# Latent attention with the rotated dimensions in three blocks of 64, two heads to a query tile, and the context product on quarters of the array

## The chip, the cores and the metric

The kernel runs on one core of one Trainium2 chip. Its engines are TensorE (PE, with its weight loads PEld), VectorE (DVE), ScalarE (ACT), GpSimd (POOL) and SyncE (SP, which only issues loads here). The metric is the device time of one execution in microseconds (us). Lower is better.

## The reference

The reference is a two-layer block over x (4 batches of 256 rows, 256 wide) and a context of 4 x 256 rows, 64 wide. The first layer has a top-k attention against the context and a routed feed-forward layer. The second has a latent attention and a mixture of experts. Only the latent attention is touched here. For each of its H = 16 heads, in words:

```
q     = norm(x) @ Wq_h.T                    # 128 wide
c     = q @ w_kc_q_h                        # 192 wide, latent query
c     = rope(c)                             # 192 dimensions: pairs (j, j + 96) are turned
qc    = c @ W_qr_h @ W_kr_h.T               # back to the 64 of the context
p     = softmax(qc @ rope(ctx).T)
out  += (p @ ctx') @ (w_kc_kv_h, Wo_h)      # folded
```

The rotation is x * cos + rotate_half(x) * sin with halves of 96 dimensions.

## The kernel before, in words

The weights of a pair of heads are folded first, so that the rows of x see one product less: `CH`, `CL` (Wq times w_kc_q, as two f16 parts, 256 x 2 x 192), `M` (W_qr times W_kr, 96 x 4 x 64) and `NH`, `NL` (w_kc_kv times Wo). `fold_product`, `fold_keep` and `fold_rest` (L135 to L182) do this in six parts, f = 0 to 5, through one PSUM bank; f = 0, 1 and 5 are split in two f16 parts, the high part by ACT and the remainder by DVE. `load_pair` (L188) issues 7 loads per pair from SP. The folds of pairs 0 and 1 run in the first stage (`stage_first_layer`), those of pair p+2 during pair p.

`stage_latent_attention` (L792) works through 8 pairs of heads. A pair has 8 steps t, one for each tile of 128 rows of x. Each engine has its own instruction list in a fixed order, joined by semaphores. All of them follow `pairs` (L840): steps 2 to 7 of a pair by `step`, and steps 0 and 1 of the next pair by `cross`; six pairs run in a hardware loop (`Fori`, two pairs a turn, three turns), the last two are written out.

In a step, PE does in this order:

- `scores` (L899) of tile t: two heads, against `KH` and `KL`, four f16 matmuls of 256 columns.
- `queries` (L875) for the next pair: group t of 8. A group is one head, one half of 96 dimensions and 512 rows of x: six f16 matmuls of 512 columns into 96 rows of bank 0 or 1. It waits for the rotation of the group before last.
- at steps 1 and 6 `to_context` (L888): from the rotated queries `RO` (96 rows) and `M` to 64 rows per head, four f32 matmuls of 512 columns, the two heads on the two column halves of the array, into bank 2. It serves half of the rows of x, so a pair has two calls.
- from step 3 on one part of the fold of pair p+2, the sixth in `cross` at step 0, through bank 7.
- at 3, 5, 7 and at the next pair's step 1 `attend` (L916), f32, and last `turn` (L908), four f32 transposes of the softmax rows of the tile before.

DVE does in a step: `lowest` (L1108, the minimum of the scores), the Q remainders and fold remainders where they fall, `rotate` (L1073, two products of a query group with cos and sin, 96 x 512 each, read from PSUM), `attended` (L1101) and last `inverse` (L1114), the reciprocal of the sum of the exponentials. The rotation thus stands between the minimum and the inverse, while ACT makes the exponentials (`softmax`, L986, two instructions with a sum read after each). ACT also copies Q (`to_context`, L980), the folds, the turned rows (`turned`, L995) and the attended context. POOL multiplies by the inverse (`normalise`, L1052) and adds and subtracts the rotated parts (`rotated`, L1044, two instructions after each second step), with two sets of `TM`.

The rope tables `cosq` and `sinq` are 96 x 2 x 256 each and come by two loads (L311, L312) in the first stage, ahead of three loads for the shared expert (L314) and of the loads of pairs 0 and 1.

Of the kernel before, what the change touches and what calls it, by code (L numbers as in the profile page):

```python
# [14 lines left out]
ALU = mybir.AluOpType  # L15
# [119 lines left out]
def fold_product(pe, g, u, f, o):  # L135

    if f < 2:
        for h in range(2):
            mm = pe.matmul(o[:, h * DQ:(h + 1) * DQ], g.WQ[u][:, h, f * P:(f + 1) * P], g.WCQ[u][:, h, :],
                           start=True, stop=True)  # L140
    elif f == 2:
        for h in range(2):
            pe.transpose(o[:, h * HALF:(h + 1) * HALF], g.WQR[u][:, h, :, :].rearrange("j a r -> j (a r)"),
                         g.ident[0:HALF, 0:HALF])
        mm = pe.transpose(o[:, 2 * HALF:2 * HALF + DC], g.WKR[u][:, :, :].rearrange("d h r -> d (h r)"),
                          g.ident[0:DC, 0:DC])
    elif f == 3:
        for h in range(2):
            for c in range(KT):
                mm = pe.transpose(o[:, h * D + c * P:h * D + (c + 1) * P], g.WO[u][:, c, h * HK:(h + 1) * HK],  # L150
                                  g.ident[:, :])
    elif f == 4:
        for h in range(2):
# [10 lines left out]
def fold_keep(act, g, r, u, f, o):  # L164
# [3 lines left out]
    if f == 2:  # L168
        act.activation(g.RT[:, 0, :], o[0:R, 0:2 * HALF + DC], ACT.Copy)
        return act.activation(g.RT[:, 1, :], o[R:P, 0:2 * HALF + DC], ACT.Copy)  # L170
    if f == 3:
        return act.activation(g.WOT[:, :, :], o, ACT.Copy)
    if f == 4:
        return act.activation(g.M[u][:, :, :], o[0:HALF, 0:4 * DC], ACT.Copy, scale=1.0 / UP)
# [10 lines left out]
DW = 7 * 16  # L185


def load_pair(sp, g, i, r, u):  # L188

    two_heads = bass.ds(2 * r, 2)  # L190
    wqr_v = i["L1_xattn_W_qr"].rearrange("h (a j) r -> j h a r", a=2)
    sp.dma_start(g.WQ[u][:, :, :], i["L1_xattn_Wq"].rearrange("(h k) n -> k h n", k=HK)[:, two_heads, :]
                 ).then_inc(g.d_w[u], 16)
    sp.dma_start(g.WCQ[u][:, :, :], i["L1_xattn_w_kc_q"].rearrange("h k q -> k h q")[:, two_heads, :]
                 ).then_inc(g.d_w[u], 16)
    sp.dma_start(g.WCV[u][:, :, :], i["L1_xattn_w_kc_kv"].rearrange("h k d -> k h d")[:, two_heads, :]
                 ).then_inc(g.d_w[u], 16)
    for h in range(2):
        sp.dma_start(g.WQR[u][:, h, :, :], wqr_v[:, bass.ds(2 * r + h, 1), :, :]).then_inc(g.d_w[u], 16)
# [6 lines left out]
def stage_first_layer(nc, g, i):  # L206
# [8 lines left out]
    with ExitStack() as ctx:  # L215
# [64 lines left out]
        fold_bank = lambda k: g.ps[:, (N_FOLD + k) % 4, :]  # L280

# [11 lines left out]
        with nc.Block() as block:  # L293
            @block.sync
            def _(sp):
# [15 lines left out]
                sp.dma_start(g.cosq[:, :, :], i["cosq"]).then_inc(g.d_ropeq, 16)  # L311
                sp.dma_start(g.sinq[:, :, :], i["sinq"]).then_inc(g.d_ropeq, 16)  # L312
# [64 lines left out]
            def _(pe):  # L377
# [91 lines left out]
                def fold(k):  # L469
# [6 lines left out]
                    fold_product(pe, g, r, f, fold_bank(k)).then_inc(filled, 1)  # L476
# [82 lines left out]
            def _(act):  # L559
# [41 lines left out]
                for n in range(3):  # L601
                    act.activation(g.shT[:, n, :, :], bank(N_SH + n), ACT.Copy,
                                   scale=UPW if n == 2 else 1.0).then_inc(emptied, 1)
                def fold(k):
# [3 lines left out]
                    if f in FOLD_SPLIT:  # L608
                        w = 2 * DQ if f < 2 else D
                        fold_keep(act, g, r, r, f, o).then_inc(fold_a, 1)  # L610
# [4 lines left out]
                    else:  # L615
                        fold_keep(act, g, r, r, f, o).then_inc(emptied, 1)
# [175 lines left out]
def stage_latent_attention(nc, g, i):  # L792
# [12 lines left out]
    with ExitStack() as ctx:  # L805
# [4 lines left out]
        TM = two("TM", [HALF, 4, 512])  # L810
        RO = sb("RO", [HALF, 2, 2, 2, 512])
# [9 lines left out]
        FIRST, AHEAD = 5, 6  # L821
        QA, QP, SC, PTB, CXB, FO = 0, 2, 3, 5, 6, 7
# [7 lines left out]
        EXP0, ROPE0, TPS0, TOK0, CXPS0, CXOK0, QC0, QCPS0, SUM0, FOLD0 = 2, 2, 2, 1, 2, 1, 1, 2, 4, 1  # L830
# [9 lines left out]
        def pairs(eng, step, cross):  # L840

            for t in HEAD:
                step(0, 0, t, True, False)
            with eng.Fori(0, (PAIRS - 2) // 2, 1) as it:
                for u in range(2):
                    for t in TILES:
                        step(it * 2 + u, u, t, True, True)
                    for t in HEAD:
                        cross(it * 2 + (u + 1), 1 - u, t, True, True)
            for t in TILES:  # L850
                step(PAIRS - 2, 0, t, True, False)
            for t in HEAD:
                cross(PAIRS - 1, 1, t, False, False)
            for t in TILES:
                step(PAIRS - 1, 1, t, False, False)

        with nc.Block() as block:
# [9 lines left out]
            def _(pe):  # L867
                def fold(r, u, f):
# [4 lines left out]
                    fold_product(pe, g, u, f, g.ps[:, FO, :]).then_inc(fold_ps, 1)  # L873

                def queries(q, u, t):  # L875

                    n, h, a = t // 4, t // 2 % 2, t % 2
                    pe.wait_ge(rope_ok, 8 * q + (t - 1 + ROPE0))
                    pe.wait_ge(fold_ok, 6 * q + (2 + FOLD0))
                    for k in range(KT):  # L880
                        for m, (cx, xx) in enumerate(split(g.CH[u], g.CL[u], g.XH, g.XL)):
                            mm = pe.matmul(g.ps[0:HALF, QA + a, :],  # L882
                                           cx[:, k, h * DQ + a * HALF:h * DQ + (a + 1) * HALF],
                                           xx[:, k, 512 * n:512 * n + 512], start=(k == 0 and m == 0),
                                           stop=(k == KT - 1 and m == 2))
                    mm.then_inc(q_ps, 1)

                def to_context(q, u, n):  # L888

                    pe.wait_ge(sum_ok, 8 * q + (4 * n + 4 + SUM0))  # L890
                    pe.wait_ge(fold_ok, 6 * q + (5 + FOLD0))
                    pe.wait_ge(qc_ok, 2 * q + (n + QC0))
                    for a in range(2):
                        for h in range(2):
                            mm = pe.matmul(g.ps[DC * h:DC * h + DC, QP, :], g.M[u][:, 2 * h + a, :],  # L895
                                           RO[:, n, h, a, :], start=(a == 0), stop=(a == 1))
# [32 lines left out]
                def step(p, u, t, asks, folds):  # L929
                    scores(p, u, t)  # L930
                    if asks:
                        queries(p + 1, 1 - u, t)
                    else:
                        shares(t)
                    if t == 1:
                        to_context(p, u, 1)
                    if t == AHEAD and asks:
                        to_context(p + 1, 1 - u, 0)
                    if folds and t >= 3:
                        fold(p + 2, u, t - 3)  # L940
# [5 lines left out]
                def cross(p, u, t, asks, folds):  # L946

                    scores(p, u, t)
                    if asks:
                        queries(p + 1, 1 - u, t)  # L950
                    else:
                        if t == 0:
                            pe.wait_ge(rope_ok, 8 * PAIRS + ROPE0)
                            pe.wait_ge(cx_ok, 4 * p - 2 + CXOK0)
                        shares(t)
                    if t == 0:
                        if folds:
                            fold(p + 1, 1 - u, FOLDS - 1)
                        turn(p - 1, LAST)
                    else:  # L960
                        to_context(p, u, 1)
# [4 lines left out]
                for t in range(NT):  # L966
                    queries(0, 0, t)
                    if t == FIRST:
                        to_context(0, 0, 0)
# [5 lines left out]
            def _(act):  # L975
                def fold(r, u, f):
                    act.wait_ge(fold_ps, 6 * r + (f + 1))
                    fold_keep(act, g, r, u, f, g.ps[:, FO, :]).then_inc(fold_hi if f in FOLD_SPLIT else fold_ok, 1)

                def to_context(q, u, n):  # L980
                    act.wait_ge(qc_ps, 2 * q + (n + 1 + QCPS0))
                    for h in range(2):
                        act.activation(Q[h][u][HI[h], 512 * n:512 * n + 512], g.ps[HI[h], QP, :],  # L983
                                       ACT.Copy).then_inc(qc_hi, 1)
# [22 lines left out]
                def step(p, u, t, asks, folds):  # L1007
                    softmax(p, t)
                    if t == 1:
                        to_context(p, u, 1)  # L1010
                    if t == AHEAD and asks:
                        to_context(p + 1, 1 - u, 0)
                    if folds and t >= 3:
                        fold(p + 2, u, t - 3)
# [5 lines left out]
                def cross(p, u, t, asks, folds):  # L1020

                    softmax(p, t)
                    if t == 0:
                        if folds:
                            fold(p + 1, 1 - u, FOLDS - 1)
                        turned(p - 1, LAST)
                    else:
                        to_context(p, u, 1)
# [4 lines left out]
                to_context(0, 0, 0)  # L1033
# [5 lines left out]
            def _(pool):  # L1039
# [4 lines left out]
                def rotated(q, st):  # L1044

                    n, h, tm = st // 2, st % 2, TM[st % 2]
                    pool.wait_ge(rope_ok, 8 * q + (2 * st + 2 + ROPE0))
                    pool.wait_ge(qc_ps, 2 * q + (n + QCPS0 - 1))
                    pool.tensor_tensor(RO[:, n, h, 0, :], tm[:, 0, :], tm[:, 2, :], ALU.subtract).then_inc(sum_ok, 1)  # L1049
# [705 lines left out]
```

## Time and profile before

| | |
|---|---|
| time, three runs | 531.78 us median (531.44 to 533.56) |
| profiled execution: its own time | 531.13 us |
| its span, first to last instruction | 529.4 us |
| mean granted TensorE clock | 0.973 |
| PE busy | 490.2 us (93%) |
| DVE busy | 321.7 us (61%) |
| ACT busy | 245.5 us (46%) |
| POOL busy | 182.1 us (34%) |

The attention stage runs from about 137 to 388 us, with six of its pairs in the hardware loop. Times in the rows are us from the start of the span. A matmul's duration includes its way through the array, so matmuls that follow each other overlap: the distance of their starts is what one costs. An f32 matmul leaves two records. "xN" is the number of records in a row.

### The profile page before, as it was taken

How to read it: one execution, taken by the hardware profiler on the slowest of the kernel's cores; microseconds unless marked ns; L12 is line 12 of the kernel's file. 1: busy time of each engine (PE TensorE's matmuls, PEld its weight loads, DVE VectorE, ACT ScalarE, POOL GpSimd, SP SyncE). 2: the span in 40 equal slices, each digit the busy share in tenths (PEclk: the TensorE clock that was granted, in tenths of full speed). 3: DMA queues.
4: the chain of work that ended last, by engine and by line, in shares of the span. 5: the costliest groups of instructions: out<-in, count | busy, mean ns of one | idle time of the engine just before them, and what ended most of it. 6: DMA issues, size and time to landing. Idle time of an engine off the chain costs nothing. (4 is left out here: it accounts for less than half of the span.)

```text
span 529.4 us, 9451 instructions
## 1 busy us (share of the span) xinstructions
PE 490.2 (93%) x3202; PEld 345.2 (65%) x3202; DVE 321.7 (61%) x881; ACT 245.5 (46%) x596; POOL 182.1 (34%) x181
## 2 busy tenths in 40 slices
PE   4988989987789999999999999999989879999997
PEld 2776878775336566556656565656766546999986
DVE  4989799732477677676867676675465790322102
ACT  3674364643026666566666667656634300332200
POOL 3141311302157566665666566674410000000000
PEclk9997999999699999999999999999989979999999
DMA  8813000000000020202001000000069000087002
GB/s 266 230 55 92 2 1 1 1 1 1 0 1 1 2 71 0 72 0 56 13 14 55 0 0 0 0 1 1 2 163 285 1 1 1 21 260 228 2 0 80
DMA packets 41298, 26.25 MB, mean 50 GB/s; under 512 B 10048, under 2 KB 40816, under 8 KB 41264
## 3 DMA queue, kind: packets, MB, share of 16 engines
q1 hardware_dynamic: 41264, 25.81, 16.8%
q8 instruction: 20, 0.33, 0.3%
q14 instruction: 14, 0.11, 0.1%
HBM read 24.75 MB, written 1.05 MB: 49 GB/s over the span
## 5 line engine op out<-in xcount | busy, mean ns | idle before, releaser
L1055 POOL TENSOR_TENSOR PB<-PB,inv 128x512 f32<-128x512 f32 x64 | 66.5, 1039 | 89.8 <-DVE inv L1117 89.3
L990 ACT ACTIVATE PB<-ps,low 128x256 f32<-128x256 f32 x128 | 59.6, 471 | 48.0 <-DVE low L1111 48.0
L1111 DVE TENSOR_REDUCE low<-ps 128x2 f32<-128x512 f32 x64 | 43.9, 685 | 31.6 <-PE ps L904 30.8
L1082 DVE TENSOR_TENSOR TM<-ps,cosq 96x512 f32<-96x512 f32 x64 | 43.9, 686 | 22.6 <-PE ps L882 21.1
L882 PE MATMUL ps<-XH,CH 128*96 128x512 f16 x128 | 49.8, 389 | 2.7 <-POOLq L1042 2.6
L882 PE MATMUL ps<-XL,CH 128*96 128x512 f16 x128 | 49.5, 387 | 0.0
L882 PE MATMUL ps<-XH,CL 128*96 128x512 f16 x128 | 49.5, 387 | 0.0
L1049 POOL TENSOR_TENSOR RO<-TM 96x512 f32<-96x512 f32 x32 | 40.5, 1267 | 21.4 <-DVE TM L1083 21.4
L1083 DVE TENSOR_TENSOR TM<-ps,sinq 96x512 f32<-96x512 f32 x64 | 43.3, 677 | 0.0
L912 PE MATMUL ps<-ident,PB 128*128 128x128 f32 x256 | 40.6, 281 | 1.8 <-POOL PB L1055 1.1
L358 POOL TENSOR_TENSOR HT<-GL,MS 128x512 f32<-128x512 f32 x16 | 20.3, 1277 | 63.6 <-ACT MS L630 48.7
L912 PEld LDWEIGHTS ps<-ident,PB 128*128 128x128 f32 x256 | 28.4, 141 | 19.6 <-issue 10.5
L1050 POOL TENSOR_TENSOR RO<-TM 96x512 f32<-96x512 f32 x32 | 40.6, 1269 | 0.0
L998 ACT ACTIVATE PTS<-ps 128x512 f32<-128x512 f32 x64 | 38.2, 598 | 3.7 <-PE ps L912 2.0
L983 ACT ACTIVATE Q<-ps 64x512 f16<-64x512 f32 x32 | 18.9, 592 | 35.1 <-PE ps L895 34.7
L921 PE MATMUL ps<-PTS,KV 128*64 128x256 f32 x256 | 34.3, 389 | 0.7 <-ACT PTS L998 0.7
L539 PE MATMUL ps<-XT,W1T 128*128 128x256 f32 x128 | 32.9, 409 | 0.0
L904 PE MATMUL ps<-KH,Q 128*128 128x256 f16 x128 | 31.4, 273 | 1.5 <-DVE Q L1097 1.5
L895 PE MATMUL ps<-RO,M 96*64 96x512 f32 x128 | 31.0, 605 | 1.6 <-POOL RO L1050 1.6
L904 PE MATMUL ps<-KL,Q 128*128 128x256 f16 x128 | 31.4, 273 | 0.0
L505 PE MATMUL ps<-W2T,HT 128*128 128x256 f32 x128 | 29.3, 383 | 0.2
L539 PEld LDWEIGHTS ps<-XT,W1T 128*128 128x128 f32 x128 | 25.2, 204 | 4.0
(220 smaller groups left out, 973.3 us busy)
## 6 DMA issues: line engine op xcount, KB each, us to landing
EG<-in_L_ffn_W_gate_dram SPq DMA_DIRECT2D x10, 384.0 KB, 4.3
EU<-in_L_ffn_W_up_dram SPq DMA_DIRECT2D x10, 384.0 KB, 5.1
ED<-in_L_ffn_W_down_dram SPq DMA_DIRECT2D x10, 384.0 KB, 5.7
w<-in_L_ffn_W_dram SPq DMA_DIRECT2D x2, 1024.0 KB, 8.5
WQ<-in_L_xattn_Wq_dram SPq DMA_DIRECT2D x8, 256.0 KB, 2.8
WO<-in_L_xattn_Wo_dram SPq DMA_DIRECT2D x8, 256.0 KB, 3.1
WCQ<-in_L_xattn_w_kc_q_dram SPq DMA_DIRECT2D x8, 192.0 KB, 2.7
X<-in_x_dram SPq DMA_DIRECT2D x2, 512.0 KB, 4.1
```

What stands on the lines that cost most here:

```text
L539: mm = pe.matmul(g.ps[:, HB + u % 2, S * o:S * o + S], W1T[:, k, (2 * n + o) * P:(2 * n + o + 1) * P], XT[b % 2][:, k, :], start=(k == 0), ...
L882: mm = pe.matmul(g.ps[0:HALF, QA + a, :], cx[:, k, h * DQ + a * HALF:h * DQ + (a + 1) * HALF], xx[:, k, 512 * n:512 * n + 512], start=(k = ...
L904: mm = pe.matmul(g.ps[:, SC + t % 2, S * h:S * h + S], Q[h][u][:, t * P:(t + 1) * P], kx[:, S * (t // 2):S * (t // 2) + S], start=(m == 0) ...
L912: mm = pe.transpose(g.ps[:, PTB, j * P:(j + 1) * P], PB[t % 2][:, j // 2, (j % 2) * P:(j % 2 + 1) * P], g.ident[:, :])
L990: e = act.activation(PB[t % 2][:, h, :], g.ps[:, SC + t % 2, h * S:(h + 1) * S], ACT.Exp, bias=low[:, t % 2, h:h + 1], scale=-1.0, accum_o ...
L998: act.activation(PTS[t // 2 % 2][:, :, (t % 2) * P:(t % 2 + 1) * P], g.ps[:, PTB, :].rearrange("p (j n) -> p j n", j=4), ACT.Copy).then_in ...
L1049: pool.tensor_tensor(RO[:, n, h, 0, :], tm[:, 0, :], tm[:, 2, :], ALU.subtract).then_inc(sum_ok, 1)
L1050: pool.tensor_tensor(RO[:, n, h, 1, :], tm[:, 3, :], tm[:, 1, :], ALU.add).then_inc(sum_ok, 1)
L1055: pool.tensor_tensor(PB[t % 2][:, :, :], PB[t % 2][:, :, :], inv[:, t % 2, :].unsqueeze(2).broadcast_to([P, 2, S]), ALU.mult).then_inc(nor ...
L1082: dve.tensor_tensor(batches(TM[st % 2][:, c, :]), src, over(g.cosq[:, a, :]), ALU.mult)
L1083: dve.tensor_tensor(batches(TM[st % 2][:, s, :]), src, over(g.sinq[:, 1 - a, :]), ALU.mult).then_inc(rope_ok, 1)
L1111: dve.tensor_reduce(low[:, t % 2, :], g.ps[:, SC + t % 2, :].rearrange("p (h s) -> p h s", h=2), AX.X, ALU.min).then_inc(low_ok, 1)
```

## The change

The 192 rotated dimensions of a head are laid out in three blocks of 64, and the two heads stand side by side in one tile of 128 columns of `CH`. Block 0 is dimensions 0 to 63, block 1 is 96 to 159, and block 2 holds what is left of both halves (64 to 95 and 160 to 191). A query group is now one block, both heads and 512 rows of x, in all 128 rows of a bank: six groups per pair for eight (`queries`, `rotate`). Blocks 0 and 1 are turned as before, by two POOL instructions. For block 2, DVE writes the products with cos and sin straight to `RO`, as blocks 2 and 3, and `M` has the exchange of the halves in it; sin has its sign in the table. `M` has 4 blocks, with head 0 in rows 0 to 63 and head 1 in rows 64 to 127 (`fold_product` f = 4, in eight matmuls of 64 x 64 for four of 64 x 96, into banks 7 and 2).

`to_context` becomes one call per pair: 4 blocks x 2 halves of the rows x 2 heads, each on a quarter of 64 x 64 of the array, with head 0 into bank 2 and head 1 into bank 7. As bank 7 is also the folds', PE waits at step 6 for all folds of pair p+2, and fold 0 for the end of the Q remainders. ACT copies all four pieces of Q at the end of its step 6. DVE does the remainders in two parts, before and after the inverse of step 7.

The steps are reordered: folds on PE at steps 0 to 5; queries at steps 7 and 0 to 4; DVE takes the inverse before it rotates; the remainder of fold 5 stands on DVE at step 6 after the inverse. `TM` is single, with 128 rows. The hardware loop is gone: all eight pairs are written out. The loads per pair are 13 (w_kc_q in 4, W_qr in 5), those of the tables 12 for 2; in the first stage ACT negates half of the sin table's third block, in two instructions.

```diff
+BLOCKS = 4
+CUTS = (0, DC, 2 * DC, 2 * DC + DC // 2)
+RTW = 2 * DC + 3 * DC // 2
...
     elif f == 4:
-        for h in range(2):
-            for a in range(2):
-                mm = pe.matmul(o[0:HALF, (2 * h + a) * DC:(2 * h + a + 1) * DC],
-                               g.RT[:, a, h * HALF:(h + 1) * HALF], g.RT[:, h, 2 * HALF:2 * HALF + DC],
+        for k, c in enumerate(CUTS):
+            for h, bank in enumerate((o, other)):
+                rows = slice(DC * h, DC * h + DC)
+                mm = pe.matmul(bank[rows, DC * k:DC * k + DC], g.RT[rows, c:c + DC], g.RT[rows, RTW:RTW + DC],
                                start=True, stop=True)
...
-DW = 7 * 16
+DW = 13 * 16
+ROPE_LOADS = 12 * 16
...
             for t in HEAD:
-                step(0, 0, t, True, False)
-            with eng.Fori(0, (PAIRS - 2) // 2, 1) as it:
...
+                step(0, 0, t, True, True)
+            for p in range(PAIRS):
+                for t in TILES:
+                    step(p, p % 2, t, p < PAIRS - 1, p < PAIRS - 2)
+                if p < PAIRS - 1:
                     for t in HEAD:
+                        cross(p + 1, 1 - p % 2, t, p < PAIRS - 2, p < PAIRS - 3)
...
+                def queries(q, u, k):
+                    n, j = k // 3, k % 3
+                    pe.wait_ge(rope_ok, 6 * q + (k - 1 + ROPE0))
...
+                            mm = pe.matmul(g.ps[:, QA + k % 2, :], cx[:, c, j * P:(j + 1) * P],
+                                           xx[:, c, 512 * n:512 * n + 512], start=(c == 0 and m == 0),
+                                           stop=(c == KT - 1 and m == 2))
...
+                def to_context(q, u, folded):
+                    pe.wait_ge(rope_ok, 6 * q + (6 + ROPE0))
+                    pe.wait_ge(sum_ok, 4 * q + (4 + SUM0))
+                    pe.wait_ge(fold_ok, 6 * q + (folded + FOLD0))
+                    pe.wait_ge(qc_ok, 2 * q + QC0)
+                    for k in range(BLOCKS):
+                        for n in range(2):
+                            for h in range(2):
+                                rows = HI[h]
+                                mm = pe.matmul(g.ps[HI[n], QP[h], :], g.M[u][rows, k, :], RO[rows, k, n, :],
+                                               start=(k == 0), stop=(k == BLOCKS - 1))
                     mm.then_inc(qc_ps, 1)
...
                     scores(p, u, t)
+                    if not asks:
                         shares(t)
+                    elif t <= 4:
+                        queries(p + 1, 1 - u, t + 1)
+                    elif t == AHEAD:
+                        to_context(p + 1, 1 - u, 12 if folds else 6)
+                    elif t == LAST and folds:
+                        queries(p + 2, u, 0)
+                    if folds and t < FOLDS:
+                        fold(p + 2, u, t)
                     if t in (3, 5, 7):
                         attend(p, t // 2 - 1)
                     if t >= 1:
                         turn(p, t - 1)
...
                     softmax(p, t)
+                    if folds and t < FOLDS:
+                        fold(p + 2, u, t)
                     if t in (3, 5, 7):
                         attended(p, t // 2 - 1)
                     if t >= 1:
                         turned(p, t - 1)
+                    if t == AHEAD and asks:
+                        to_context(p + 1, 1 - u)
...
                     lowest(p, t)
+                    if folds and t in (1, 2):
+                        fold(p + 2, u, t - 1)
                     if t == LAST and asks:
                         to_context(p + 1, 1 - u, 0)
+                    inverse(p, t)
+                    if asks and t < GROUPS_Q:
+                        rotate(p + 1, t)
+                    if folds and t == FOLDS:
+                        fold(p + 2, u, FOLDS - 1)
+                    if t in (4, 6):
+                        attended(p, t // 2 - 2)
+                    if t == LAST and asks:
+                        to_context(p + 1, 1 - u, 1)
```

## Rows read from the trace of the kernel before

**Rows 1.** Windows, one pair: us, busy of PE, PEld, DVE, ACT, POOL, clock, DMA.

```profile
186.10:215.90 29.80, 29.80 (x190) 18.22 (x188) 21.41 (x44) 19.07 (x56) 18.14 (x17) 1.00 0.12 32
```

**Rows 2.** Timeline of SP: first load of a pair, three pairs.

```profile
186.09 0.40 SPq L192 DMA_DIRECT2D WQ<-in_L_xattn_Wq_dram  x1
...
215.85 0.40 SPq L192 DMA_DIRECT2D WQ<-in_L_xattn_Wq_dram  x1
...
246.15 0.38 SPq L192 DMA_DIRECT2D WQ<-in_L_xattn_Wq_dram  x1
```

**Rows 3.** Timeline in the attention stage: start us, us, engine, line, operation.

```profile
243.44 0.27 PE L904 MATMUL ps<-KH,Q 128*128 128x256 f16 x1
...
243.88 0.38 PE L882 MATMUL ps<-XH,CH 128*96 128x512 f16 x1
...
244.08 0.69 DVE L1111 TENSOR_REDUCE low<-ps 128x2 f32<-128x512 f32 x1 [0.65 <-PE ps L904]
...
244.81 0.47 ACT L990 ACTIVATE PB<-ps,low 128x256 f32<-128x256 f32 x1 [0.57 <-DVE low L1111]
244.96 0.38 PE L882 MATMUL ps<-XH,CL 128*96 128x512 f16 x1
...
245.27 0.65 PE L160 MATMUL ps<-WOT,WCV 128*64 128x256 f32 x4
...
245.63 0.20 ACT L990 ACTIVATION_READ_ACCUMULATOR PB<-ps,low 128x1 f32 x1
...
245.85 0.66 PE L912 MATMUL ps<-ident,PB 128*128 128x128 f32 x4
...
248.17 1.94 PE L895 MATMUL ps<-RO,M 96*64 96x512 f32 x8
...
248.88 0.68 DVE L1083 TENSOR_TENSOR TM<-ps,sinq 96x512 f32<-96x512 f32 x1
...
249.48 0.15 DVE L1117 RECIPROCAL inv<-tot 128x2 f32<-128x2 f32 x1
...
249.93 1.04 PE L921 MATMUL ps<-PTS,KV 128*64 128x256 f32 x8
...
250.90 0.66 PE L912 MATMUL ps<-ident,PB 128*128 128x128 f32 x4
...
333.03 0.27 PE L904 MATMUL ps<-KH,Q 128*128 128x256 f16 x1
...
360.05 0.27 PE L904 MATMUL ps<-KH,Q 128*128 128x256 f16 x1
```

**Rows 4.** Groups of instructions: out<-in xcount, busy us, mean ns of one.

```profile
L882 PE MATMUL ps<-XH,CH 128*96 128x512 f16 x128 | 49.8, 389 | 2.7 <-POOLq L1042 2.6
...
L1097 DVE TENSOR_TENSOR Q<-ps,Q 64x512 f16<-64x512 f32 x26 | 17.9, 689 | 0.6
L983 ACT ACTIVATE Q<-ps 64x512 f16<-64x512 f32 x24 | 14.2, 592 | 15.0 <-PE ps L895 14.7
...
L182 DVE SCALAR_TENSOR_TENSOR NL<-ps,NH 128x256 f32 x6 | 2.4, 400 | 0.0
```

**Rows 5.** Timeline of PE in the first stage: serial f32 matmuls.

```profile
58.47 7.17 PE L505 MATMUL ps<-W2T,HT 128*128 128x256 f32 x32
```

**Rows 6.** Timeline of SP and PE in the first stage.

```profile
20.20 0.60 SPq L202 DMA_DIRECT2D WO<-in_L_xattn_Wo_dram  x1
...
30.23 1.54 PE L139 MATMUL ps<-WCQ,WQ 128*128 128x192 f32 x8
```

**Rows 7.** Windows around idle TensorE and half clock.

```profile
11.50:13.50 2.00, 0.00 (x0) 0.00 (x0) 2.00 (x9) 1.97 (x3) 1.86 (x3) 1.00 0.96 361
...
129.80:132.20 2.40, 0.00 (x0) 0.00 (x0) 2.06 (x8) 0.20 (x1) 0.00 (x0) 0.96 0.00 0
132.40:136.90 4.50, 1.08 (x4) 0.71 (x4) 1.38 (x3) 0.60 (x1) 0.00 (x0) 0.50 0.00 0
...
388.00:391.60 3.60, 3.60 (x19) 2.60 (x18) 2.82 (x12) 1.32 (x2) 1.73 (x9) 0.53 0.45 123
```

More of the change, by code:

```diff
@@ L603, in _ @@
                                    scale=UPW if n == 2 else 1.0).then_inc(emptied, 1)
+                act.wait_ge(g.d_ropeq, ROPE_LOADS)
+                for h in range(2):
+                    rows = slice(DC * h + DC // 2, DC * h + DC)
+                    act.activation(g.sinq[rows, 2, :], g.sinq[rows, 2, :], ACT.Copy, scale=-1.0)
                 def fold(k):
@@ L927, in shares, with step @@
                     output_share(pe, g, t // 2, range(0, 4) if t % 2 == 0 else range(4, PAIRS - 1))
-                def step(p, u, t, asks, folds):
+                def step(p, u, t, asks=True, folds=True):
                     scores(p, u, t)
-                    if asks:
-                        queries(p + 1, 1 - u, t)
-                    else:
+                    if not asks:
                         shares(t)
[L935 to L940, printed above, removed]
+                    elif t <= 4:
[6 more added lines that the diff above has]
+                        fold(p + 2, u, t)
                     if t in (3, 5, 7):
@@ L965, in _ @@
                 pe.wait_ge(credit, 1)
[L966 to L969, printed above, removed]
+                for k in range(GROUPS_Q):
+                    queries(0, 0, k)
+                queries(1, 1, 0)
+                to_context(0, 0, 12)
                 pairs(pe, step, cross)
@@ L1005, in attended, with step @@
                                    ACT.Copy).then_inc(cx_hi, 1)
-                def step(p, u, t, asks, folds):
+                def step(p, u, t, asks=True, folds=True):
                     softmax(p, t)
[L1009 to L1014, printed above, removed]
+                    if folds and t < FOLDS:
+                        fold(p + 2, u, t)
                     if t in (3, 5, 7):
@@ L1127, in step, with cross @@
+                def cross(p, u, t, asks=True, folds=True):
+                    lowest(p, t)
+                    if folds and t == 1:
+                        fold(p + 2, u, 0)
+                    inverse(p, t)
                     if asks:
                         rotate(p + 1, t)
-                    if t in (4, 6):
-                        attended(p, t // 2 - 2)
-                    inverse(p, t)
-                def cross(p, u, t, asks, folds):
-                    lowest(p, t)
-                    if asks:
-                        rotate(p + 1, t)
-                    if t == 0:
-                        attended(p - 1, B - 2)
-                    inverse(p, t)
-                    if t == 0 and folds:
-                        fold(p + 1, 1 - u, FOLDS - 1)
-                    if t == 1:
-                        attended(p - 1, B - 1)
@@ L1146, in _ @@
-                dve.wait_ge(credit, 1)
-                dve.wait_ge(g.d_ropeq, 32)
-                for t in range(NT):
-                    rotate(0, t)
-                    if t == FIRST + 1:
-                        to_context(0, 0, 0)
+                    attended(p - 1, B - 2 + t)
+                dve.wait_ge(credit, 1)
+                dve.wait_ge(g.d_ropeq, ROPE_LOADS)
+                for k in range(GROUPS_Q):
+                    rotate(0, k)
+                for n in range(2):
+                    to_context(0, 0, n)
```

198 lines of the change are left out of this document (96 added, 102 removed).

## The prediction

> **What bounds the kernel now.** The table of the page names TensorE (PE) as the busiest engine, but that is an average over stages, so the windows come next. Over one whole pair of heads PE is busy for all 29.8 us, at clock 1.00; VectorE (DVE) is busy 21.4 us, GpSimd (POOL) 18.1 us [rows 1]. The weight loads of the pairs start at 186.09, 215.85 and 246.15 us: 29.8 us a pair, 30.3 where the loop jumps back [rows 2]. So a pair is PE's own work laid end to end, with the others in its shadow. The timeline shows the pieces [rows 3]: scores 0.44 us (243.44 to 243.88), matmuls of a query group 0.216 us apart (five steps from 243.88 to 244.96), so 1.29 us a group. Each has a record of 0.38, so 0.17 of it is a tail that costs PE nothing. Fold 5 is 0.58 (245.27 to 245.85), a turn 0.49 (0.66 less the tail), a context call 1.76 (248.17 to 249.93), an attend 0.97 (to 250.90).
>
> The profiled execution took 531.13 us, 0.65 below the median of 531.78; the sum is made on 531.13.
>
> **Queries.** Eight groups of six matmuls become six groups. 12 matmuls fewer per pair at 0.216 us are 2.6 us, on the path now; 96 over eight pairs (of 3 x 128 [rows 4]) are **20.7 us**. DVE loses four rotations of 2 x 0.61 (one product from 248.88 to the next instruction at 249.48), POOL four sums; 128 rows for 96 cost nothing, since the minimum over 128 rows takes 0.69 and the product over 96 rows 0.68 [rows 3].
>
> **Context product.** Before, two calls of four f32 matmuls. Column halves already run together: the two products of fold 5 are done in 0.65 - 0.17 (tail) = 0.48 us, while 16 serial ones of the same 256 columns take 7.17, 0.45 each [rows 3, 5]. So a call is two rounds of 0.88. After, 16 matmuls of 64 x 64: four rounds if quarters run in fours, 4 x 0.88 + 0.1 = 3.6 us, as the two calls before; eight rounds if the row halves take turns, 7.0. No row shows two row halves at once. I take 3.6, by the nearest row, the column halves, which overlap almost fully. The Trainium skill (TensorE: Matmul & The Clock Gate, "Measured speedup vs the span model") gives 3.07 times for four row tiles; by that the call is an estimated 4.6 us, 1 us more per pair and 8 in all. No row here shows it. The product f=4 becomes eight quarter matmuls for four; I take the same time, bounds -0.4 and +0.8 a pair.
>
> **First new wait.** The context product now also writes the folds' bank, so at step 6 PE waits until fold 5 of pair p+2 is emptied. DVE does that in its own step 6, behind the minimum, the exponentials and the inverse of the scores that PE has just issued. From PE free to PE free: 0.20 to the minimum (243.88 to 244.08), 0.73 to the exponentials (244.81), 1.02 for them (to 245.83), 0.05, inverse 0.08 (its 0.15 less overlap), remainder NL 0.40, handover 0.05: **2.5 us** [rows 3, 4]. PE's queue is in order: turn 5, scores 7 and the next query group stand behind it, and ACT's turned(5) waits for them.
>
> **Second.** DVE used to rotate while ACT made the exponentials; now it waits for them, takes the inverse and then rotates. A step of it is 0.73 + 1.02 + 0.05 + 0.08 + 1.22 = 3.1 us, with attended (256 columns, as NL) 3.4. PE's steps 0, 2, 4 and 5 would be 2.9, 2.8, 3.1 and 2.5 us by the pieces above, so DVE sets the pace there, and PE waits: query group k needs rotation k-2, scores t the exponentials t-2, the turn the normalised rows. POOL runs behind the inverse and has room, as it is busy 18.1 of 29.8 us and loses four sums [rows 1].
>
> **Third.** Four copies of Q on ACT (0.59 each; turned(5), twice the rows and as many columns, is put at 0.6) stand between turned(5) and the exponentials of step 7, and DVE's second remainder pair (2 x 0.69) between inverse(7) and the next pair [rows 4].
>
> **The path round a pair**, end to end. DVE steps 0, 2, 4, 5: 3.4, 3.1, 3.4, 3.1. Steps 1 and 3, where PE is longer (scores, queries, fold, attend, turn: 0.44 + 1.29 + 0.5 to 0.7 + 0.97 + 0.5, with handovers): 4.05 each. Step 6 to the emptied fold: 2.3 (2.5 less the 0.2 before the minimum, since DVE comes to it late). Context 3.6. Then turn with tail 0.7, turned 0.6, copies 2.4, exponentials 1.02, inverse 0.13, remainders 1.35: 6.2. Sum 3.4 + 4.05 + 3.1 + 4.05 + 3.4 + 3.1 + 2.3 + 3.6 + 6.2 = **33.2 us**, against 29.8: +3.4 a pair. The 2.6 us of queries are in this already. The order of before, laid out with the same durations, gives 29.7, so the method holds for it. Handovers 0.02 us shorter or longer move the pair by 0.5.
>
> **Total of the loop.** Six pairs with folds: +20.4. Pair 6 took 27.0 (333.03 to 360.05) [rows 3]; it has no folds and no fold wait, so 33.2 less PE's hole of 3.3 (2.5, and 0.8 by which DVE lags in the layout): 29.9, +2.9. Pair 7: 0. Prologue: seven query groups for eight -1.3, whole context product for half +1.8, twice the copies and remainders +1: +1.5. Written-out loop: two jumps of 0.5 fewer, -1.0 [rows 2]; longer straight code costs 0 to 2, taken as 0, since straight code of the first stage runs 32 records in 7.17 us without a hole [rows 5]. Sum **+23.8**.
>
> **First stage.** SP issues 10 loads more for the tables and 6 more for pair 0; the last of pair 0 went out at 20.20 us, and at 0.5 us each goes out at 28.2, landing near 32, while the first fold began at 30.23 [rows 6]. That is 0 to 3 us on a path that DVE's top-k shares; taken **+1**. The same 13 loads inside the loop (under 8 us) are asked for almost a pair ahead: hidden. If that cover went, it would be some 3 us a pair.
>
> **Clock.** Before 132.2 us PE stood 2.4 us and its granted clock fell from 2.4 to 1.2 GHz; it stood 2.0 us from 11.5 and the clock stayed; a short half-clock stretch lasts 3.6 us (388.0) [rows 7], in which 1.8 are lost. The new hole of about 3.3 us is longer than the one after which it fell. Half of six pairs gives **+5**, bounds 0 and 20 (each time, the whole context product at half clock).
>
> The Trainium skill (TensorEngine Tiling (Array Packing), "Key Properties") says that a change of tiling mode drains the engine. The trace agrees with a small price, 0.1 us before fold 5 and before the context call. By it the one call for two saves 0.2 us a pair.
>
> 531.13 + 23.8 + 1 + 5 = **561 us**.
>
> **Rivals.** *Row halves take turns*: the context call is 7.0 us, +3.4 on the path of each of eight pairs, 27 more: **588**. For it: no row shows them together. Against: they use separate rows and separate banks, and column halves overlap. Chance 0.15.
>
> *The clock falls in every pair*: +20 in place of +5: **576**. For it: the fall after 2.4 us. Against: the stay after 2.0, and dense work behind the hole. Chance 0.12.
>
> *Faster*: DVE's new order is not the pace. PE's attends and turns cover its longer steps, and only the wait for fold 5 is paid: 531.1 - 20.7 + 6 x 2.5 - 1.0 = **524.4**. What decides is whether the way from one context product to the next by ACT and DVE (6.2 + 23.4 = 29.6 us) is longer than PE's own work meanwhile (29.8 - 2.6 - 3.6 = 23.6). For it: DVE is busy 21.4 of 29.8 us now and loses 4.9 us of work. Against: 1.1 us of each of its eight steps, now used, becomes waiting. Chance 0.06.
>
> **How the numbers follow.** The forecast has 0.67, its own range 546 to 572 (clock, first stage, handovers). The range given is 546 to 590: it takes in the clock case and most of the case of the row halves, and leaves out the faster case and the edges. A measurement of this kernel can tell about 0.5% from no change. The forecast and two rivals lie above that; faster has 0.05, within 0.5% 0.03, slower 0.92.
>
> **What would show it.** Right: loads of the pairs 33 us apart; PE idle some 3 us before the context product, released by DVE's NL remainder; that product's 32 records in 3.6 to 3.8 us; DVE idle about 1.1 us before each reciprocal, released by ACT; 288 query matmuls. Wrong: pairs under 30 us; a context call of 7 us; half clock in each pair; first folds much after 30 us.

## The result and the profile after

The changed kernel takes 568.41 us (median of 4 runs, 561.34 to 570.54) against 531.61 for the kernel before; the ratio is 1.065, with a 95% interval of 1.054 to 1.076. It is slower by 37 us. The forecast was 561, with a range of 546 to 590. The profiled execution took 567.87 us.

The page of the changed kernel, engines first, then the granted clock by fortieths of the span:

```profile
span 566.2 us, 9137 instructions
...
PE 487.3 (86%) x3306; PEld 330.4 (58%) x3306; DVE 301.7 (53%) x849; ACT 244.0 (43%) x598; POOL 143.6 (25%) x149
...
PEclk9986999997899898999979989899999989999999
```

Every engine is busy for less time than in the table of before, ACT only a little (244.0 us for 245.5), and all are idle for longer. PE went from 93% to 86%. So no added work is the cost. It must be waits and the lower clock.

The pairs of heads, by their first weight load (timeline of SP; [rows 2] before):

```profile
178.50 0.41 SPq L201 DMA_DIRECT2D WQ<-in_L_xattn_Wq_dram  x1
...
214.44 0.39 SPq L201 DMA_DIRECT2D WQ<-in_L_xattn_Wq_dram  x1
...
249.42 0.39 SPq L201 DMA_DIRECT2D WQ<-in_L_xattn_Wq_dram  x1
...
284.05 0.39 SPq L201 DMA_DIRECT2D WQ<-in_L_xattn_Wq_dram  x1
```

A pair takes 35.9, 35.0 and 34.6 us, where it took 29.8. The last of them in windows (columns as in [rows 1]):

```profile
249.42:284.05 34.63, 29.40 (x202) 16.25 (x203) 18.91 (x40) 18.85 (x55) 13.28 (x13) 0.95 0.12 28
```

PE stands still for 5.2 of the 34.6 us, and its clock is no longer 1.00. The groups of instructions say what stands still (the last two columns are idle time just before, and its releaser):

```profile
L920 PE MATMUL ps<-RO,M 64*64 64x512 f32 x256 | 41.1, 796 | 22.4 <-DVE NL L189 19.3 <-issue 2.0 <-DVE RO L1113 1.0
...
L1146 DVE RECIPROCAL inv<-tot 128x2 f32<-128x2 f32 x64 | 10.6, 165 | 62.4 <-ACT PB L1016 62.4
```

The context product waits 19.3 us in six places for NL, the remainder of fold 5. The reciprocal waits 62.4 us for the exponentials; in the kernel before it was 6.6:

```profile
L1117 DVE RECIPROCAL inv<-tot 128x2 f32<-128x2 f32 x64 | 9.8, 153 | 6.7 <-ACT PB L990 6.6
```

The timeline of step 6 of one pair shows the first wait link by link:

```profile
251.18 0.27 PE L929 MATMUL ps<-KL,Q 128*128 128x256 f16 x1
...
252.17 0.68 DVE L1140 TENSOR_REDUCE low<-ps 128x2 f32<-128x512 f32 x1
...
252.88 0.47 ACT L1016 ACTIVATE PB<-ps,low 128x256 f32<-128x256 f32 x1 [1.00 <-DVE low L1140]
...
253.94 0.17 DVE L1146 RECIPROCAL inv<-tot 128x2 f32<-128x2 f32 x1 [1.09 <-ACT PB L1016]
254.02 0.40 DVE L189 SCALAR_TENSOR_TENSOR NL<-ps,NH 128x256 f16<-128x256 f32 x1
...
254.68 5.05 PE L920 MATMUL ps<-RO,M 64*64 64x512 f32 x32 [3.22 <-DVE NL L189]
```

PE has issued its last score matmul at 251.18, and the context product starts at 254.68, as soon as NL is out. By the handover of before (0.20 us from PE free to the minimum) the minimum could have started at 251.5, but DVE is behind with its rotation and starts at 252.17. This is the lag that the forecast had put at 0.8 us; it is 0.7. The product then takes 5.05 us, not 3.66. The windows around it give the reason (columns as in [rows 1]):

```profile
251.50:254.60 3.10, 0.00 (x0) 0.00 (x0) 2.01 (x6) 1.40 (x5) 2.31 (x3) 0.92 0.46 91
254.60:257.70 3.10, 3.02 (x16) 1.16 (x20) 0.15 (x1) 0.00 (x0) 0.62 (x1) 0.53 0.17 38
257.70:259.60 1.90, 1.90 (x20) 0.47 (x12) 0.00 (x0) 0.00 (x0) 0.00 (x0) 1.00 0.42 102
```

PE does nothing for 3.2 us, and its granted clock falls from 2.4 to 1.2 GHz near the end of this and stays there for about 3 us of the product. That happened in all six pairs with such a hole: the six products take 6.38, 5.36, 5.05, 6.49, 5.36 and 5.10 us. Against the 3.66 of the product at full clock that is 11.8 us. Pair 6 has two shorter holes, 2.30 us before a query group and 2.03 before the last product, and there the clock stayed up.

The whole: the attention (first query matmul to last attend) went from 249.4 us (136.94 to 386.3) to 285.3 (139.38 to 424.7), +36.0. Of this 11.8 are the clock and 24.2 the waits, less what the change saves. It begins 2.4 us later, and the stage behind it is 1.6 us shorter; the experiment with the tables comes back to the later start.

### The profile page after: what moved, and what is told of

Same layout as the page of the kernel before. It is cut to its first block and busy times, and to the rows that moved or that the text cites. A ratio compares the mean times of both kernels' runs of the same rounds, so it can differ in the third digit from the quotient of the medians.

```text
span 566.2 us, 9137 instructions
## 1 busy us (share of the span) xinstructions
PE 487.3 (86%) x3306; PEld 330.4 (58%) x3306; DVE 301.7 (53%) x849; ACT 244.0 (43%) x598; POOL 143.6 (25%) x149
## 5 line engine op out<-in xcount | busy, mean ns | idle before, releaser
L920 PE MATMUL ps<-RO,M 64*64 64x512 f32 x256 | 41.1, 796 | 22.4 <-DVE NL L189 19.3
L905 PE MATMUL ps<-XH,CH 128*128 128x512 f16 x96 | 37.8, 394 | 16.2 <-DVE TM L1113 11.5
L1146 DVE RECIPROCAL inv<-tot 128x2 f32<-128x2 f32 x64 | 10.6, 165 | 62.4 <-ACT PB L1016 62.4
L920 PEld LDWEIGHTS ps<-RO,M 64*64 64x64 f32 x256 | 13.7, 179 | 44.9 <-issue 43.4
L905 PE MATMUL ps<-XL,CH 128*128 128x512 f16 x96 | 37.4, 390 | 0.0
L905 PE MATMUL ps<-XH,CL 128*128 128x512 f16 x96 | 37.4, 390 | 0.0
L770 DVE MAX8 m<-work 128x8 f32<-128x256 f32 x72 | 26.7, 410 | 0.0
L905 PEld LDWEIGHTS ps<-XH,CH 128*128 128x128 f16 x96 | 9.6, 100 | 29.3 <-DVE TM L1113 15.0
L946 PEld LDWEIGHTS ps<-PTS,KV 128*64 128x64 f32 x256 | 16.2, 136 | 17.7 <-issue 7.9
```

The source lines that it names most:

```text
L905: mm = pe.matmul(g.ps[:, QA + k % 2, :], cx[:, c, j * P:(j + 1) * P], xx[:, c, 512 * n:512 * n + 512], start=(c == 0 and m == 0), stop=(c ...
L920: mm = pe.matmul(g.ps[HI[n], QP[h], :], g.M[u][rows, k, :], RO[rows, k, n, :], start=(k == 0), stop=(k == BLOCKS - 1))
L946: mm = pe.matmul(g.ps[DC * h:DC * h + DC, CXB, 0:S], g.KV[:, 2 * b + j, 0, :], PTS[b % 2][:, 2 * h + j, :], start=(j == 0), stop=(j == 1))
```

## Experiments

Ratios are to the kernel before, in runs on the same chip. Times of different kernels are also compared directly; the kernel before took 530.6 to 531.6 us (medians) beside them, so such a difference is good to about 1 us. The first four kernels are the changed one with one thing altered.

**Fold 5 emptied a step earlier.**

```diff
-                    if folds and t == FOLDS:
+                    if folds and t == FOLDS - 1:
                         fold(p + 2, u, FOLDS - 1)
```

> The changed kernel with one edit: DVE empties fold 5 at the end of its step 5 instead of step 6. My theory (the hole before the context product is the wait for this emptying, 3.2 us, and it also makes the clock fall): the releaser NL goes away; the next wait in the same place is POOL's last sum of the rotation, released behind the inverse of step 5, and the hole shrinks to about 2.3 us. Pairs get 1.1 us shorter (7 us over six pairs), and fewer pairs have half clock, up to 8 us more: 553 to 561 us. The rival theory, that DVE's order alone sets the pair and the hole is only where it shows: no gain, 566 to 570.

Measured: 557.99 us, ratio 1.051 (1.048 to 1.054). The wait for NL is gone, and another stands in its place:

```profile
L920 PE MATMUL ps<-RO,M 64*64 64x512 f32 x256 | 37.8, 740 | 15.3 <-POOL RO L1074 12.2 <-issue 3.1
```

The hole is 2.04 us where it was 3.22, released by POOL's last sum. Of the six products in a pair with folds, two now run at full clock throughout (3.66 us) and four take 5.36. The attention is 8.8 us shorter in the profiles (276.5 for 285.3): 7.1 us of waiting and 5.0 of clock less, and about 3.4 lost in pair 6, where the clock now fell behind both of its holes (2.30 and 2.04 us), as it had not in the changed kernel. So the wait for fold 5 is a cause, but with it gone the pair is still over 32 us.

**Rotation before the inverse on DVE**, in `step` and, in the same way, in `cross`.

```diff
-                    inverse(p, t)
                     if asks and t < GROUPS_Q:
                         rotate(p + 1, t)
+                    inverse(p, t)
```

> The changed kernel with one edit: DVE rotates before it takes the inverse, as in the kernel before, so that its rotation runs beside ACT's exponentials. My theory (1.2 us of waiting stand in each of DVE's six steps with a rotation): the wait of the reciprocal for ACT falls from 62 us to about 25, pairs go from 34.7 to about 32, the hole stays near 2.5 us, 543 to 550 us. If only the wait for fold 5 counts: the time stays within 2 us of 568.

Measured: 541.04 us, ratio 1.024 (1.017 to 1.031). It is the larger cause. The time falls by 27 of the 37 us:

```profile
L920 PE MATMUL ps<-RO,M 64*64 64x512 f32 x256 | 32.7, 653 | 18.6 <-DVE NL L189 15.5 <-issue 2.1 <-DVE RO L1113 1.0
...
L1146 DVE RECIPROCAL inv<-tot 128x2 f32<-128x2 f32 x64 | 10.1, 158 | 22.3 <-ACT PB L1016 22.3
```

The wait for the exponentials fell from 62.4 to 22.3 us, and the hole from 3.22 to 2.56 us, since DVE no longer comes late to step 6. The clock now fell in one of the six pairs only, and in pair 6, 1.7 us each; so 8.4 of the 27 us are clock that came back, not waiting. The theory that only fold 5 counts is out.

**The hole filled.**

```diff
                     elif t == AHEAD:
+                        if folds:
+                            pe.wait_ge(rope_ok, 6 * (p + 1) + (5 + ROPE0))
+                            for w in range(14):
+                                pe.matmul(g.ps[:, QA, :], g.CH[1 - u][:, 0, 0:P], g.XH[:, 0, 0:512], start=True, stop=True)
                         to_context(p + 1, 1 - u, 12 if folds else 6)
```

> The changed kernel with 14 additional matmuls of 512 columns (3.0 us) on PE between the scores of step 6 and the context product, into a bank that nobody reads then. They fill the hole without changing what it waits for. If the lower clock behind the hole costs time, the granted clock stays at 1.00 in all pairs, the context product takes 3.7 us in each instead of 5 or more, pairs 33.3 us instead of 34.2 to 35.9, 556 to 560 us. If the clock does not matter, the matmuls cost nothing or up to 1 us a pair: 568 to 574.

Measured: 560.21 us, ratio 1.053 (1.048 to 1.058). 84 matmuls more make the kernel 8 us faster. The loads of its pairs, and its products:

```profile
213.78 0.39 SPq L201 DMA_DIRECT2D WQ<-in_L_xattn_Wq_dram  x1
...
247.07 0.39 SPq L201 DMA_DIRECT2D WQ<-in_L_xattn_Wq_dram  x1
...
280.33 0.39 SPq L201 DMA_DIRECT2D WQ<-in_L_xattn_Wq_dram  x1
```

```profile
219.05 3.67 PE L920 MATMUL ps<-RO,M 64*64 64x512 f32 x32 [0.21 <-DVE NL L189]
...
252.33 3.66 PE L920 MATMUL ps<-RO,M 64*64 64x512 f32 x32 [0.21 <-DVE NL L189]
```

Pairs take 33.3 us with the clock up (33.29 and 33.26), the products 3.66. The waiting for NL is as long as before, but PE is at work in it. So the clock is worth 1.3 to 2.7 us a pair, and the rest of the slowdown stays. Pair 6 had no filling, and there the clock fell behind both holes, as in the first experiment, which costs about 3.4 us. 11.8 less 3.4 is 8.4 us, and the attention is 8.4 us shorter (276.9 us).

**Tables behind the pair loads.** The 12 loads of the rope tables are moved behind those of pairs 0 and 1, and the change of sign to the end of ACT's first stage:

```diff
-                half = DC // 2
-                for h in range(2):
...
                 for r in range(2):
                     load_pair(sp, g, i, r, r)
+                half = DC // 2
+                for h in range(2):
...
                 norm_root(act, g, n2, B - 1)
                 second_norm(B - 1)
+                act.wait_ge(g.d_ropeq, ROPE_LOADS)
```

> The changed kernel with the 12 loads of the rope tables issued behind those of pairs 0 and 1, and the change of sign of the sine table at the end of ACT's first stage. If the first stage is longer by the late weights of pair 1 (2.2 us of waiting), the attention starts 2.4 us earlier and the time is 565 to 566. If the delay is hidden by the rest of the stage: 568.

Measured: 565.26 us (563.33 to 572.6), ratio 1.070 (1.062 to 1.078). Against the spread of the changed kernel itself this settles nothing. The attention began at 132.6 us, but in other kernels with the old first stage it began anywhere from 134.4 to 141.4. It is taken up again below, on a kernel that varies less.

**Inverse first, in the kernel before.** One part of the change alone; `cross` is altered in the same way.

```diff
                     lowest(p, t)
...
+                    inverse(p, t)
                     if asks:
                         rotate(p + 1, t)
                     if t in (4, 6):
                         attended(p, t // 2 - 2)
-                    inverse(p, t)
```

> The kernel before with one part of the change alone: DVE takes the inverse before it rotates. If this order costs time by itself, also where PE has 29.8 us of work in a pair, the wait of the reciprocal for ACT grows from 7 us to about 50 us, pairs go from 29.8 to 30.4 us and the time by 3 to 5 us: 534 to 536. If it costs only in the changed kernel, where PE's steps are shorter: 530 to 531, no change.

Measured: 540.41 us, ratio 1.019 (1.014 to 1.025). The direction is that of the theory, the size is double. The reciprocal:

```profile
L1117 DVE RECIPROCAL inv<-tot 128x2 f32<-128x2 f32 x64 | 10.6, 166 | 48.2 <-ACT PB L990 47.7
```

```profile
PE ps L139 <- DVE CL L182: 4.8, 6, 1.2
...
PE ps L143 <- DVE CL L182: 2.4, 6, 0.4
```

The wait grew from 6.6 to 47.7 us, as expected. What the estimate had missed are the folds: PE waits 4.8 and 2.4 us for the remainders CL (list of waits: total, times, longest), which DVE now reaches too late and which PE's matmuls did not wait for before. Together 7.2 us; the attention is 7.9 us longer in the profile (257.3 for 249.4), and it began 1.0 us later. So of the 9.6 us measured about 8 are the order, even where PE has its full work.

**Both edits.** Fold 5 early and rotation first, in the changed kernel.

> The changed kernel with both edits, fold 5 emptied in DVE's step 5 and rotation before the inverse. If the two causes add up, it is faster than rotation first alone (541) by 3 us of waiting and what half clock was left: 535 to 538, still above the kernel before, because PE now waits before the context product for POOL's last sum (2.0 us a pair). If fold 5 was only the visible part: 541.

Measured: 535.9 us (531.91 to 543.82), ratio 1.008 (1.005 to 1.011). The two take away 32.5 of the 37 us. By themselves they took 10.4 and 27.4; both got back some of the same loss of clock. What is left before the product:

```profile
L920 PE MATMUL ps<-RO,M 64*64 64x512 f32 x256 | 31.0, 624 | 14.3 <-POOL RO L1074 11.2 <-issue 2.1 <-DVE RO L1113 1.0
```

1.86 us a pair wait for POOL's last sum. The six query groups end one step before the product needs all of them, and what they save is still spent in this and other waits.

**Order made anew.** All of the change kept (in `cross` and ahead of the first pair it is altered to match, not shown), with the query groups moved forward, fold 5 early, rotation first, and the copies of Q split over two steps:

```diff
-                    elif t <= 4:
-                        queries(p + 1, 1 - u, t + 1)
+                    elif t <= 3:
+                        queries(p + 1, 1 - u, t + 2)
                     elif t == AHEAD:
                         to_context(p + 1, 1 - u, 12 if folds else 6)
-                    elif t == LAST and folds:
-                        queries(p + 2, u, 0)
+                    elif t in (5, LAST) and folds:
+                        queries(p + 2, u, 0 if t == 5 else 1)
...
                     softmax(p, t)
+                    if t >= AHEAD and asks:
+                        to_context(p + 1, 1 - u, (t - AHEAD,))
...
-                    if asks and t in (1, 2):
-                        rotated(p + 1, 0, t - 1)
-                    if asks and t in (4, 5):
-                        rotated(p + 1, 1, t - 4)
+                    if asks and t in (0, 1):
+                        rotated(p + 1, 0, t)
+                    if asks and t in (3, 4):
+                        rotated(p + 1, 1, t - 3)
...
-                    inverse(p, t)
-                    if asks and t < GROUPS_Q:
-                        rotate(p + 1, t)
-                    if folds and t == FOLDS:
+                    if asks and t < GROUPS_Q - 1:
+                        rotate(p + 1, t + 1)
+                    if folds and t == AHEAD:
+                        rotate(p + 2, 0)
+                    inverse(p, t)
+                    if folds and t == FOLDS - 1:
                         fold(p + 2, u, FOLDS - 1)
```

> All parts of the change kept (six query groups, quarters, loop written out), with the order made anew: fold 5 emptied in step 5, rotation first, the first query groups of a pair in steps 5 and 7 of the pair before, so that the last rotated sum is ready at step 6, and ACT's copies of Q split over steps 6 and 7 directly behind the exponentials. If the orders alone made the change slow, and the 2.6 us of queries per pair are real, pairs take 27.2 to 27.7 us, the hole before the context product goes and the clock stays at 1.00: 514 to 520 us, faster than both. If the quarters or the 13 loads cost as well: 526 to 532.

Measured: 516.18 us (514.71 to 518.0), ratio 0.972 (0.969 to 0.975). It is 15 us faster than the kernel before and 52 faster than the changed one, with the same instructions but for their order:

```profile
203.04 0.39 SPq L201 DMA_DIRECT2D WQ<-in_L_xattn_Wq_dram  x1
...
230.62 0.39 SPq L201 DMA_DIRECT2D WQ<-in_L_xattn_Wq_dram  x1
...
258.15 0.39 SPq L201 DMA_DIRECT2D WQ<-in_L_xattn_Wq_dram  x1
```

```profile
L920 PE MATMUL ps<-RO,M 64*64 64x512 f32 x256 | 29.3, 595 | 0.0
...
L1147 DVE RECIPROCAL inv<-tot 128x2 f32<-128x2 f32 x64 | 10.2, 159 | 17.7 <-ACT PB L1017 17.4
```

A pair takes 27.5 us, and nothing waits before the product. The difference to 29.8 is 2.3 us, near the 2.6 us of twelve matmuls. So the new form of the computation brings nearly what it removes, and the quarters and the added loads cost at most 0.3 us a pair. The attention takes 235.5 us for 249.4. That is 13.9 us, of 20.7 forecast for the queries alone; where the rest went was not followed. The loop written out was not tested by itself; by the jumps in [rows 2] it is worth 1 us.

**Rows of the array by turns.** The changed kernel with all of head 0 before head 1.

```diff
-                    for k in range(BLOCKS):
-                        for n in range(2):
-                            for h in range(2):
+                    for h in range(2):
+                        for k in range(BLOCKS):
+                            for n in range(2):
```

> The changed kernel with the loops of the context product in another order: all matmuls of head 0 (rows 0 to 63 of the array), then all of head 1. Same matmuls and banks. If four quarters really run at once only because neighbours in the list lie on different quarters, the product now runs two at a time: the first one at full clock takes 7 us instead of 3.7, pairs get 3.4 us longer, 590 to 600 us. If the order of the list does not matter: 3.7 us and 568.

Measured: 587.19 us, ratio 1.103 (1.098 to 1.109). That is less than the 590 to 600 expected and more than 568. The list order matters, but the first product, at full clock, takes neither 3.7 nor 7 us:

```profile
155.44 5.43 PE L920 MATMUL ps<-RO,M 64*64 64x512 f32 x32 [1.04 <-DVE RO L1113]
```

The weight loads of this product, in one timeline (xN is how many in a row):

```profile
156.32 0.17 PEld L920 LDWEIGHTS ps<-RO,M 64*64 64x64 f32 x2 [0.26 <-issue]
156.75 0.17 PEld L920 LDWEIGHTS ps<-RO,M 64*64 64x64 f32 x2 [0.26 <-issue]
157.18 0.23 PEld L920 LDWEIGHTS ps<-RO,M 64*64 64x64 f32 x6 [0.26 <-issue]
157.61 0.23 PEld L920 LDWEIGHTS ps<-RO,M 64*64 64x64 f32 x4 [0.20 <-issue]
...
159.42 0.14 PEld L920 LDWEIGHTS ps<-RO,M 64*64 64x64 f32 x2 [0.29 <-issue]
```

Loads come every 0.43 us, by twos at first, by fours or more in the middle, by twos at the end. So the 32 records take about 12 slots of 0.43 us instead of 8 (in the changed order) or 16. It looks as if the second head starts before the first has ended; the records do not name the quarter, so this is read from the doubled loads, not shown. The later products take 7.1 to 8.8 us, a large part of it at half clock.

**Two small ones on the reordered kernel.** The tables' loads behind the pair loads (same edit as above), and the product's loops as block, head, half:

> The reordered kernel (516 us) with the loads of the rope tables behind those of pairs 0 and 1 as well. In the reordered kernel PE waits 1.2 and 2.5 us in the first stage for the weights of pair 0 and pair 1. If that delay reaches the end of the first stage, the attention starts 2 to 3 us earlier and the time is 513 to 514. If the rest of the stage hides it: 516, with the spread of the starts (134 to 141 us in runs of the same first stage) as before.

Measured: 513.01 us (512.8 to 513.93), ratio 0.966 (0.964 to 0.969). The first folds no longer wait:

```profile
29.88 1.54 PE L145 MATMUL ps<-WCQ,WQ 128*128 128x192 f32 x8
...
35.81 1.57 PE L145 MATMUL ps<-WCQ,WQ 128*128 128x192 f32 x8
```

In the reordered kernel they start at 31.12 and 39.65 us. The attention begins at 132.67 us for 135.86 and takes 235.5 us in both, so the gain is all in the first stage. This is the fastest of all versions, 18 us below the kernel before; how much that kernel would gain by another order of its loads was not tried.

The spread of the starts has a second source. TensorE waits 2.0 to 3.2 us at 36 to 39 us for the weights of pair 1, and in six of the eight executions the granted clock falls behind this wait. Windows of the kernel with rotation first, the changed one and the one with the hole filled:

```profile
36.00:56.00 20.00, 16.06 (x120) 12.67 (x120) 18.19 (x73) 10.44 (x22) 6.16 (x7) 1.00 0.42 108
...
36.00:56.00 20.00, 17.32 (x82) 12.88 (x82) 16.18 (x69) 8.52 (x18) 4.27 (x5) 0.66 0.43 108
...
36.00:56.00 20.00, 16.17 (x72) 12.36 (x72) 13.44 (x60) 7.68 (x18) 3.16 (x4) 0.57 0.41 100
```

Their attention begins at 134.38, 139.38 and 141.40 us. With the tables' loads moved back the wait is gone and the clock in this window is 1.00, in both kernels. So these loads cost a wait and, in some executions, clock. This is read from profiled executions; no run separates the two.

```diff
                     for k in range(BLOCKS):
-                        for n in range(2):
-                            for h in range(2):
+                        for h in range(2):
+                            for n in range(2):
```

> The reordered kernel with the four quarter matmuls of a block issued as head 0 twice, then head 1 twice, in place of alternating heads. If all four that overlap only have to be near in the list, the context product stays at 3.66 us and the time at 516. If neighbours must be on different row halves, it takes 4 to 5.4 us and the time is 520 to 530.

Measured: 515.08 us (2 runs), ratio 0.970 (0.965 to 0.975), the product 3.66 us. Within a block the order of the four quarters is free.

## Why the prediction was right, point by point

**Queries, -20.7 us.** Right in kind: 288 query matmuls. The saving shows only where nothing waits, 27.5 us a pair in the reordered kernel for 29.8.

**Context product, 3.6 us if quarters run in fours.** Right at full clock: 3.66 us with its tail, in the first and the last of the eight products; the six between took 5.05 to 6.49. The rival of the row halves is out. The Trainium skill's 3.07 times for four row tiles (TensorE: Matmul & The Clock Gate, "Measured speedup vs the span model") would have given an estimated 4.6; for row halves together with column halves, this case shows 4 x 0.88.

**First new wait, 2.5 us, 3.3 with DVE's lag.** Right: 3.22 us, and 2.56 when the lag is taken away.

**Second, DVE's order.** Right, and the larger part. The reciprocal's wait is 1.08 or 1.09 us in 45 of 64 steps, as forecast, and 0.62 or 0.86 in the others.

**The path round a pair, 33.2 us.** Right: 33.3 us with the clock kept up by filling matmuls. Without the clock's part the attention grew by 24.2 us (36.0 less 11.8), and the forecast of the loop was 23.8.

**Clock, +5 us.** This is the term that was mis-sized. I took the clock to fall in half of the six pairs and 1.8 us each time; it fell in all six and cost 2.0 us each, 11.8 us in all. With 11.8 in its place, the attention's forecast of +28.8 (23.8 + 5) becomes +35.6; 36.0 were measured. "Half clock in each pair" was one of my signs of being wrong, and it came; pairs of 34.6 to 35.9 us, not 33, came with it. The rival of the clock in every pair was right in its count, but its 3.4 us each were too many, since the clock came back within the product.

"Half of six" rested on two rows that I misread. The hole in which the clock fell did not last 2.4 us. TensorE stood for 3.48, and the clock fell within it, at 132.0 us:

```profile
133.24 1.08 PE L104 MATMUL ps<-ident,XN 128*128 128x128 f32 x4 [3.48 <-DVE XN L95]
```

So the new hole of 3.3 us was shorter than this one, not longer. The hole of 2.0 us at 11.5 after which the clock "stayed" shows nothing. The trace has no clock record before 26 us, and four records that take 0.66 us at full clock and 1.08 in the line above at half took 1.06 here:

```profile
10.39 1.06 PE L389 MATMUL ps<-ident,CT 128*64 128x128 f32 x4
```

The engine was most likely at half clock already. Without that row, nothing spoke for a clock that stays up in half of the pairs. That the time still fell inside the range is due to the other terms, which were near.

**First stage, +1 us.** +2.4 in the profiled execution, but not on the path that I named: the first fold of pair 0 began at 29.82 us, without a wait, and it was pair 1 that waited, 2.17 us at 38. This start varies by 7 us between executions, so one of them can't say whether +1 was near. The experiment on the reordered kernel puts the loads of the tables at 3 us.

**Faster, 524.4.** Out. The way round by ACT and DVE does set the pace: with rotation put back beside the exponentials the time falls by 27 us.

## What to carry to other kernels

When work is taken off the bounding engine, lay one period of the loop end to end for every engine and see which order of waits becomes the longest way round; here the same instructions took 568 us in one order and 516 in another. A reciprocal that waits for ACT should have other work in front of it, and a buffer that two products share should be emptied a step before the second needs it. If a wait of 3 us on TensorE can't be removed, filling it with matmuls whose result nobody reads was worth 8 us here.

## What the runs showed of the hardware

In the attention's pairs with folds, the granted clock fell in or within 2.1 us behind each of the 18 holes of 3.2 us (the changed kernel, tables late, rows by turns), behind four of the six of 2.0 us (fold 5 early), one of the six of about 2.6 us (rotation first) and one of the six of 1.86 us (both edits). In pair 6 the same hole of 2.0 us let it fall in some kernels and not in others. So the length of the hole does not decide alone; what the engine did before differs between these kernels, and which part of it matters stays open.

Four f32 matmuls of 64 x 64 on different quarters run together in 0.88 us, and their order within a block is free. With all of one row half first, 16 matmuls took 5.43 us, between the 3.66 of fours and the 7 of twos.

With the first stage's code the same, the attention began at 134.4 to 141.4 us in eight profiled executions of the changed kernel and its variants; in the two with the tables' loads moved back it began at 132.6 and 132.7. The three latest (139.4, 141.0 and 141.4) are those with a mean granted clock of 0.66, 0.66 and 0.57 between 36 and 56 us; the other five had 0.83 to 1.00.
